# Second graph attention: GpSimd adds the second feed-forward bias to the normed row, and ScalarE copies the finished sums one step sooner

## What is computed

```python
h = (x @ W).reshape(N, H, HD)                      # H = 4 heads of 64
e = leaky_relu(al_src[src] + al_dst[dst], 0.2)     # per edge, self loops added
alpha = softmax over the edges into dst
y = segment_sum(alpha * h[src], dst) + gat_b
y = layernorm(y + x, ln1_g, ln1_b)
f = gelu(y @ W1 + b1) @ W2 + b2
out = layernorm(f + y, ln2_g, ln2_b)               # then a residual and a norm without gain
```

## Time and profile before

| what | value |
|---|---|
| median of 3 runs | 3915.99 us (3908.12 to 3917.78) |
| the profiled execution's own time | 3910.59 us |
| its span | 3908.7 us |
| busy over the span | PE 95%, DVE 58%, ACT 52%, POOL 14% |
| second attention, pass 1 | about 1641 to 2042 us |
| second attention, pass 2 with its last steps | about 2042 to 2545 us |
| mean TensorE clock granted | 0.98 of full speed |

### The profile page before, as it was taken

How to read it: one execution, slowest core, us unless ns; L and a number is a source line. 1 busy time by engine, 2 the same in 40 slices (tenths; PEclk the granted TensorE clock), 3 DMA queues, 4 the chain that set the end, 5 groups by cost and what they waited for, 6 DMA issues and landing times. The chain is left out here.

```text
span 3908.7 us, 69870 instructions
## 1 busy us (share of the span) xinstructions
PE 3697.8 (95%) x27513; PEld 2879.2 (74%) x27514; DVE 2283.0 (58%) x4498; ACT 2040.2 (52%) x3732; POOL 533.7 (14%) x599
## 2 busy tenths in 40 slices
PE   6999969999999999499999999889999999999999
PEld 3666647677777666377777777678888888888887
DVE  8999946556556555399999999600012221004665
ACT  3555547666666666389998999600000000003554
POOL 1000001111111111100005666500000000000000
PEclk9999979999999999699999999989999999999999
DMA  2555562333333332333352333253333333333332
GB/s 97 237 212 228 222 236 103 103 98 106 101 107 97 108 110 70 143 134 113 119 188 92 107 107 112 71 203 143 141 135 137 137 137 137 120 133 143 137 137 72
DMA packets 177220, 521.12 MB, mean 133 GB/s; under 512 B 54305, under 2 KB 141734, under 8 KB 143782
## 3 DMA queue, kind: packets, MB, share of 16 engines
q1 hardware_dynamic: 174390, 510.02, 36.9%
q10 hardware_dynamic: 2544, 7.08, 0.6%
HBM read 354.74 MB, written 162.29 MB: 132 GB/s over the span
## 5 line engine op out<-in xcount | busy, mean ns | idle before, releaser
L1737 PE MATMUL t_acc<-t_r,t_ct 128*128 128x256 f32 (+1 forms) x3750 | 856.7, 380 | 19.9 <-DMA t_r<-d_r 15.7
L975 ACT ACTIVATE a_sm<-a_p_t 128x1024 f32<-128x1024 f32 (+1 forms) x800 | 667.5, 835 | 385.1 <-PE a_p_t L913 381.5
L1737 PEld LDWEIGHTS t_acc<-t_r,t_ct 128*128 128x128 f32 x3750 | 701.9, 190 | 114.2 <-DMA t_r<-d_r 16.1
L913 PE MATMUL a_p_t<-ident,a_sm 128*128 128x128 f32 x5000 | 702.5, 280 | 54.8 <-ACT a_sm L969 33.1
L969 ACT ACTIVATE a_sm<-a_sm,a_negm 128x1024 f32<-128x1024 f32 (+2 forms) x600 | 702.0, 1170 | 62.5 <-DVE a_negm L1035 62.2
L913 PEld LDWEIGHTS a_p_t<-ident,a_sm 128*128 128x128 f32 x5000 | 562.2, 143 | 231.5 <-issue 210.6
L927 PE MATMUL a_p_o<-a_sm,a_v 128*64 128x128 f32 x10000 | 700.8, 279 | 29.8 <-ACT a_sumT L982 29.8
L927 PEld LDWEIGHTS a_p_o<-a_sm,a_v 128*64 128x64 f32 x10000 | 556.2, 137 | 209.2 <-issue 106.0
L1055 DVE CUSTOM_DVE_ANT_0 a_sm<-a_p_s,a_full 128x400 f32<-128x400 f32 x800 | 427.5, 571 | 424.4 <-PE a_p_s L899 418.6
L899 PE MATMUL a_p_s<-a_kt,a_q 64*128 64x400 f32 x1600 | 395.6, 556 | 27.5 <-DMA a_full<-d_logs 22.2
L1071 DVE SCALAR_TENSOR_TENSOR a_sm<-a_a_bc,a_al 128x3125 f32<-128x3125 f32 x100 | 346.3, 3463 | 26.0 <-DMA a_a_bc<-d_as 18.0
(11 more groups left out here) (238 smaller groups left out, 3671.2 us busy)
## 6 DMA issues: line engine op xcount, KB each, us to landing
t_ct<-d_ct SPq DMA_DIRECT2D x74, 1600.0 KB, 6.7
a_mask<-d_full SPq DMA_DIRECT2D x50, 1600.0 KB, 7.1
d_logs<-logs SPq DMA_DIRECT2D x25, 1664.0 KB, 7.0
a_full<-d_logs SPq DMA_DIRECT2D x25, 1664.0 KB
d_ct<-ct SPq DMA_DIRECT2D x25, 1600.0 KB, 5.3
d_full<-a_full SPq DMA_DIRECT2D x25, 1600.0 KB, 6.0
t_ct<-d_full SPq DMA_DIRECT2D x25, 1600.0 KB, 6.8
a_a_bc<-d_as SPq DMA_DIRECT2D x8, 1600.0 KB, 10.7
```

The costliest lines, as they stand in the source:

```text
L913: m = nc.tensor.transpose(p_t[u % 2][:, i * P:(i + 1) * P], sm[buf][:, a * P:(a + 1) * P], ident[:, :])
L975: nc.scalar.activation(sm[buf][:, a_row[u] * P:a_row[u + 1] * P], p_t[u % 2][:, 0:turns[u] * P], ACT.Copy).then_inc(s_copy, 1)
L1737: m = self.nc.tensor.matmul(self.acc[t % 2][:, 0:width], self.ct[t % 3][:, a * P:(a + 1) * P], rows[:, a, 0:width], start=a == 0, stop=a = ...
```

## The change

1. `b2` is no longer added by a product of `ones` and `b2` at the end of the product with W2. It is loaded as a row broadcast over 128 partitions, and GpSimd adds it in place to the normed row `y`, after TensorE has transposed `y`. The step comes after `rstd3` in GpSimd's order. DVE's sum at (3, 7) waits for it.
2. In an attention without dot products, `flip` of unit n runs in the body of unit n+1 at turn 3, ahead of `copy`, and not in the body of unit n+2 at turn 0.
3. The Relu copy on ACT moves from slot 6 to slot 7, so behind `normalise`.
4. The memset of `ones` and the waits for it are gone.

```diff
 def body(at):                      # ScalarE
     for u in range(ntu):
-        if u == 0 and behind(at, 2) is not None:
+        if dot and u == 0 and behind(at, 2) is not None:
             flip(behind(at, 2))
+        if not dot and u == ntu - 1 and behind(at, 1) is not None:
+            flip(behind(at, 1))
         if exists(at):
             copy(at, u)
...
-rows = {k: sb(k, [P, D]) for k in ("g1", "be1", "g2", "be2")}
-b2 = sb("b2", [1, D])
-ones = sb("ones", [1, P])
+rows = {k: sb(k, [P, D]) for k in ("g1", "be1", "g2", "be2", "b2")}
...
+PB = Steps(sem("pool_bias"), ["bias"])
...
-POOL = [("outer", 4), ("rstd1", 2), ("rstd3", 4), ("rstd2", 3)]
+POOL = [("outer", 4), ("rstd1", 2), ("rstd3", 4), ("bias", 3), ("rstd2", 3)]
...
-sp.dma_start(b2[:, :], w["b2"].rearrange("(o n) -> o n", o=1)).then_inc(s_w, 16)
...
 if (lag, s) == (3, 7):             # VectorE
+    dve.wait_ge(PB.sem, PB.at(jj, "bias"))
     dve.wait_ge(PD.sem, PD.at(jj, "down"))
...
+if what == "bias":                 # GpSimd
+    pool.wait_ge(PE_.sem, PE_.at(jj, "y"))
+    pool.tensor_tensor(y[tp][:, :], y[tp][:, :], rows["b2"][:, :], ALU.add).then_inc(PB.sem, 1)
...
 for c in range(4):                 # TensorE
-    nc.tensor.matmul(pd[:, :], zT[:, c, :], w2[:, c, :], start=c == 0, stop=False)
-nc.tensor.matmul(pd[:, :], ones[:, :], b2[:, :], start=False, stop=True).then_inc(PD.sem, 1)
+    m = nc.tensor.matmul(pd[:, :], zT[:, c, :], w2[:, c, :], start=c == 0, stop=c == 3)
+m.then_inc(PD.sem, 1)
...
-if (lag, s) == (4, 6):             # ScalarE
+if (lag, s) == (4, 7):
     act.wait_ge(DL.sem, DL.at(jj, "norm3"))
```

More of the change, by code:

```diff
@@ L1446, in pool_init @@
                 pool.memset(half_pow[:, :], -0.5).then_inc(s_init, 1)
-                pool.memset(ones[:, :], 1.0).then_inc(s_init, 1)
-                pool.wait_ge(s_init, 2)
+                pool.wait_ge(s_init, 1)
                 pool.wait_ge(s_w, n_w * 16)
@@ L1452, in pe_init @@
             def pe_init(pe):
-                pe.wait_ge(s_init, 2)
                 pe.wait_ge(s_w, n_w * 16)
```

## The result

The changed kernel takes 3919.81 us (median of 18 runs, 3917.68 to 3922.92) against 3914.77 us before (18 runs on the same chips): ratio 1.0014, 95% interval 1.0008 to 1.0021. By the medians that is 5.0 us more, a small loss, clear of the spread and inside the 0.3% that the prediction counts as "within". The forecast was 1.45 us more.

The account below looks back on a forecast made before the run. VectorE was taken to bound pass 1 and, in a loop with GpSimd, pass 2. The terms +4.0 - 1.4 - 1.55 + 0.4 = +1.45 us, on 3915.99, gave 3917.4 us; range 3908 to 3927.

Parts of the forecast that it names:

- I take it that it doesn't bar: Pass 2: the third norm (L1497, tensor_scalar, 0.41 us) shows no faster mode and doesn't hold up GpSimd's bias add.
- L1081 loses ... 0.20 us: Pass 2: GpSimd's bias add, already under way, holds VectorE's long row L1081 by 0.20 us a tile.
- the lost race: Rival, pass 2: the bias add stands until L1081 ends, delaying L1484 0.50 us a tile; 3923.4 us; chance 0.2.
- whoever starts first goes through: Pass 2: when VectorE and GpSimd rows meet, the first to start runs on and the other stands still.
- first tile, `b2` as a broadcast: First tile: `b2` loads 128 KB instead of 1 KB ahead of the second tile's loads, +0.4 us.
- 20 tiles with the add: Pass 2: 20 tiles in which the bias add costs VectorE's loop 0.20 us each, +4.0 us.
- slack, last `flip`, first `ones` at the end: Pass 2: ScalarE and TensorE's slack, -1.4 us once; at the end the last `flip` -0.65, a dropped `ones` product -0.6.
- second `flip` and `ones` at the end: End of pass 2: TensorE's wait for `flip` saves 0.4 us, the `ones` product at the next L1484 0.6.
- the last two waits: Last two tiles of pass 2: L1484 waits for the bias add, +0.35 us, twice.
- No price: Rival, pass 2: the bias add slips in between at no cost; -2.55 us, 3913.4 us; chance 0.07.
- the TensorE case: Rival, both passes: TensorE and ScalarE are the bound, so the earlier `flip` pays some -24 us, 3892 us; chance 0.08.
- the order that stalls: Rival: `flip` ahead of `copy` holds ScalarE, then TensorE's `turn`; each tenth beyond 0.5 us cover costs 2 us; chance 0.05.

Follow-up runs that it names:

- e1_flip_only: Kernel before with only the earlier `flip` and the Relu copy one slot later; `b2` stays a product with `ones`: ratio 0.9993 to before.
- e3_no_bias: Changed kernel without the bias add and VectorE's wait for it, so `b2` is not added at all: ratio 0.9992 to before.
- e5_bias_later: Changed kernel with one small GpSimd operation ahead of the bias add, so that it starts later: ratio 1.0026 to before.
- e9_pinned_sum: Kernel before with earlier `flip`, later Relu copy and second norm; GpSimd adds `be2` to the late residual row, pinned behind the residual add: ratio 0.9963 to before.
- e7_norm3_later: Changed kernel with VectorE's third norm one slot later, behind the 3125-element row: ratio 1.0028 to before.
- e2_bias_only: Changed kernel with `flip` and the Relu copy back in their old places; bias on GpSimd, no `ones` product: ratio 1.0037 to before.

## Why the prediction came out as it did

What bounds the kernel was read rightly. Pass 1 kept its length: the changed kernel lies 1.17 us behind the kernel before at the `lift` of 1675.80 and 1.20 us at that of 1912.91. Pass 2 followed VectorE's loop, and the earlier `flip` and the dropped product were worth only the slack and something at the end (e1_flip_only, e3_no_bias). Of the signs named, ScalarE's wait for `negm` in pass 2, the vanished wait for `flip` and the unchanged pass 1 came; an L1081 of 3.6 us and a period near 20.2 us didn't.

The step that failed is a size: "I take it that it doesn't bar", and with it "L1081 loses ... 0.20 us". The tensor_scalar does need what GpSimd holds. It came 0.33 us ahead of the long row, so more of the add was still to run, and it lost 0.40 us in place of 0.20. The ground for excluding it, that 0.41 us showed no faster mode, was no evidence about contention. The rule of the Trainium skill that I weighed there (SBUF — State Buffer, "Who interferes with whom") says that a tensor_scalar can contend, and the 0.81 us bear it out; the sum that I hung on it, the lost race, didn't come, because the add starts 0.07 us before the norm and not behind it. The prediction's own times had this order, 2309.68 for the add and 2309.74 for L1497: by its own rule that whoever starts first goes through, the norm had to stand, and L1497 could not bar the add. Read so, the rows of before would have given the price to the right row. That the measured time lies in the range is no merit of the 0.20: the range reached up to the lost race, whose 0.50 us a tile is near the measured 0.41.

The comparison with L1484 was also with the wrong row, because L1484 reads one of its two inputs from PSUM. The row of this size with two inputs in SBUF is L1481, 0.48 us; it was itself held once in the changed kernel, as L1479, in the first tile with the add:

```profile
2091.02 0.72 POOL L1506 TENSOR_TENSOR a_y<-a_y,a_b 128x256 f32<-128x256 f32 x1
2091.15 0.87 DVE L1479 SCALAR_TENSOR_TENSOR a_y<-a_y,a_n_rs,a_be 128x256 f32<-128x256 f32 x1 [0.52 <-POOL a_n_rs L1415]
```

It ends 0.28 us behind the add (2092.02 and 2091.74). The third norm ends 0.16 us behind the full add (2296.09 and 2295.93) and 0.15 behind the half one (2288.51 and 2288.36). So what the norm still has to do once the add is over is about half of what L1479 has, as a mode with both ports, which the prediction set aside, would make it; no run varies the mode, so this is argued and not shown.

Term by term, in the profiled executions, from the residual adds of before and after (the earlier trace rows and the rows above; the first is 2093.72 before and 2095.47 after):

| term | forecast, us | measured, us |
|---|---|---|
| first tile, `b2` as a broadcast | +0.4 | +0.1 |
| between that and the first add | not counted | +0.2 |
| 20 tiles with the add | +4.0 | 408.10 - 399.75 = +8.35 |
| one tile more, the first with the add | not counted | +0.4 |
| slack, last `flip`, first `ones` at the end | -2.65 | 7.16 - 10.10 = -2.9 |
| second `flip` and `ones` at the end | -1.0 | 5.74 - 7.16 = -1.4 |
| the last two waits | +0.7 | 6.35 - 5.74 = +0.6 |
| sum | +1.45 | +5.3 |

The numbers such as 10.10 are the shift of the same residual add between the two traces (2503.57 - 2493.47). The shift is 1.08 us where the block begins in this execution (`lift` at 1640.99 before), 1.17 behind the first tile, 1.35 ahead of the first bias add and 1.75 behind it. So the broadcast cost 0.1 us here; most of the 0.2 us comes at the change of passes, where `lift` waits for its loads in both kernels. In the last two tiles it isn't the residual add that waits, as forecast, but the third norm that is held up, 0.80 us once more; the size is the same. The spans differ by 8.8 us, of which 1.1 lie ahead of the block and 2.4 behind it; medians of 18 runs each differ by 5.0, so I count those as the spread of single executions.

The rivals: the lost race never appeared, not even where the add came later (e5_bias_later). "No price" and the TensorE case are excluded by the period. In the order of e1_flip_only ScalarE has no wait for the last `weigh` from 1680 to 2500 us, so the order that stalls is excluded too.

## What to carry over

An engine with 86% idle time isn't free if it shares a memory access with the engine that bounds the stage: price a moved operation by the row of the bounding engine that it will be running beside, and list every such row, short ones too. If the operation can be pinned by a wait beside rows that it doesn't hold, the statistics here, an add of the same size costs 0.1 in place of 0.4 us. And take work from an engine only where its time is on the bounding loop; 0.6 us a tile taken from TensorE here bought some 1.1 us in all, at the end of pass 2 (the two steps behind the last long row are 16.02 and 10.80 us in e1_flip_only, 15.65 and 10.03 in e3_no_bias).

## What the runs showed of the hardware

- A VectorE tensor_scalar on 128x256 in fp32 with two scalars per partition, SBUF to SBUF, was held up by a GpSimd tensor_tensor that started 0.07 us ahead: 0.81 in place of 0.41 us, 0.54 with half the add. Its undisturbed time is that of a two-input row of the same size (L1484, 0.41 us), although that row has an input in PSUM, so its length alone doesn't tell whether it contends.
- Statistics on 128x256 weren't held up by a GpSimd add beside them, nor the add by them: 0.43 and 0.73 us (e9_pinned_sum, 2307.22 and 2307.33), and 0.43 us too behind an add that had started first (changed kernel, 2493.87 and 2493.57).
- Even a small lead decides: GpSimd's add started 0.05 us ahead of VectorE's long row in one run (2297.40 and 2297.45, e7_norm3_later) and 0.11 us in another (2302.05 and 2302.16, e5_bias_later), and both times it went through and the long row was held.
- In the run with less work for TensorE and the late `flip` (e2_bias_only) the granted clock was below 1.00 in 9 of 23 stretches of 20 us, and eight transposes took 1.97 in place of 1.09 us; a fall made TensorE's step 21.54 in place of 19.97 us. The waits of 1.05 and 0.85 us ahead of it stand also in tiles where the clock stays.
